# Layer norm factors applied in turned layout, key tiles moved ahead of outputs, and two more feed-forward steps in the linear-attention block

## The chip, the cores and the metric

One NeuronCore of one Trainium2 chip. The metric is the device time of the whole kernel in microseconds (us), median of the runs: 906.08 us for the kernel before (three runs, 906.05 to 906.83). TensorE (PE) multiplies matrices, VectorE (DVE), ScalarE (ACT) and GpSimd (POOL) do element work, SyncE (SP) issues the DMAs.

## The reference

The input x has 2 x 1024 tokens of 256 features. Four sub-layers follow each other: a mixture of 8 experts, linear attention with a feed-forward layer, masked softmax attention, and a mixture of 16 experts. The change touches only the second:

```
qkv = x @ Wqkv + bqkv;  q, k, v = split(qkv)
qp, kp = elu(q) + 1, elu(k) + 1
kv = sum over tokens of kp^T v;   k_sum = sum over tokens of kp
attn = (qp @ kv) / (qp @ k_sum + 1e-6)
y = layer_norm(x + attn) * g1 + b1          # "the first norm"
gate, up = y @ Wg + bg, y @ Wu + bu         # 256 -> 682
ffn = (silu(gate) * up) @ Wd + bd           # 682 -> 256
out = layer_norm(y + ffn) * g2 + b2
```

## The kernel before, in words

The 2048 tokens are 16 tiles of 128 rows; a batch is 8 tiles, and 4 tiles are a group of 512 tokens (4 groups). A matrix product in fp32 accuracy is made of three products of high and low parts (`PASSES`), so each operand is needed twice: `act_hi` (the value rounded, written by ACT) and `act_lo` (the rest, written by DVE). Both hold the activations in turned layout, features on the partitions and tokens along the row, while `y` holds them with tokens on the partitions.

The program is four blocks with a barrier between them, each a hand-written list of instructions per engine with semaphores: experts 1, linear attention (`stage_linear_attention`), feed-forward (`stage_feed_forward`), and attention with experts 2. Nothing reorders instructions: what is written ahead runs ahead on its engine.

Linear attention. SP issues the load of the query bias (L869), of Wg and Wu (L871), of the remaining groups and of biases. DVE adds up the experts' two rows of a token (`combine`, L1100), PE transposes them (L953), and then for each tile `project` (L919) gives keys and values, DVE makes keys (`bias` L1124, `keys` L1130 to L1135, `values_lo` L1140), PE adds them into the batch's key-value matrix two tiles later (`keys_values`, L933). `finish` (L1146 to L1149) makes that matrix ready for use. PE's `output(i)` (L945) is numerator and denominator of tile i; DVE divides and adds into y (L1158 to L1163), takes the norm's statistics (L1153, L1168, L763); ACT takes the root (L1057), DVE the shift (`norm`, L1237 and L1238), ACT applies both (L1245). The outputs of batch 0 (tiles 0 to 7) run beside the last four tiles of batch 1, those of batch 1 (tiles 8 to 15) after `finish(1)`. Then gain and bias of the first norm are applied to whole groups as rows: POOL for groups 0 and 1 (L1089, L1091), DVE for groups 2 and 3 (L1251, L1252). PE turns the group (`turn("r", g)`, L902), ACT and DVE write its high and low part (L997, L1106). `ff_up(s)` (L774) is one of 24 up-steps of the feed-forward layer (gate and up product of 128 hidden features for one group, 12 matmuls of 128x512); steps 0 and 1 stand in this block, the others in the next.

Feed-forward. For each step ACT applies Silu (L1406), DVE makes the hidden value and its high part (`hidden`, L1522, L1528), POOL the low part (L1292). A step's PSUM banks come free when `hidden` has read them. Between `hidden(2)` and `hidden(3)` DVE splits Wd (L758, L759). After six up-steps of a group, and two of the next, stands `down(g)` (L1327), 72 products into y (L1544). POOL adds the bias rows `bd` (L1479) and `be2` (L1484) between low parts.

## Time and profile before

| quantity | value |
|---|---|
| median of 3 runs | 906.08 us (906.05 to 906.83) |
| the profiled execution | 907.32 us, of which the span 905.6 us |
| PE busy | 824.6 us, 91% |
| DVE busy | 687.1 us, 76% |
| POOL busy | 406.7 us, 45% |
| ACT busy | 363.0 us, 40% |
| granted TensorE clock, mean | 0.958 |

Times below are microseconds from the start of the span. The profile lists instructions of one engine in order of time, with the idle time just ahead of them in brackets and what ended it. The linear-attention block runs from 299.1 to 413.9, the feed-forward block from there to about 528. Shares over the whole span say little here, since each block has its own limit: PE is almost always busy in the feed-forward block and idle for a third of the last stretch of linear attention.

### The profile page before, as it was taken

What the parts mean: (1) busy time and instruction counts of PE and PEld (TensorE: products, weight loads), DVE (VectorE), ACT (ScalarE), POOL (GpSimd) and SP (SyncE); (2) the same over time, 40 slices, a digit from 0 to 9 for tenths busy, and PEclk for the clock granted to TensorE, in tenths of its full rate; (3) what the DMA queues carried; (4) which work ended last, traced back from release to release, by engine and by line L of the source; (5) the groups of instructions that cost most, each with busy time, mean ns of one, the idle gap of its engine ahead of it and who ended that gap; (6) DMA issues with size and microseconds to landing.
All of it is one profiled execution on the core that took longest, in us unless ns stands there. A gap on an engine that the chain in (4) does not pass through costs nothing. (4 is left out here: it accounts for less than half of the span.)

```text
span 905.6 us, 17121 instructions
## 1 busy us (share of the span) xinstructions
PE 824.6 (91%) x5386; PEld 737.9 (81%) x5386; DVE 687.1 (76%) x1399; ACT 363.0 (40%) x722; POOL 406.7 (45%) x482
## 2 busy tenths in 40 slices
PE   7799999999996588677999989888999999999997
PEld 4799999999995367666888879766888888888887
DVE  4887888988884477976679779786777777776776
ACT  5466556666551555243322645783111111111110
POOL 4267778777784300044786427402232323233232
PEclk9699999999998799887999999999999999999999
DMA  8336412213611700005100020010010010010002
GB/s 288 107 118 200 140 46 82 92 43 133 198 47 50 233 1 1 1 0 181 43 1 1 1 71 2 1 35 1 18 35 17 17 35 17 17 35 17 17 0 93
DMA packets 45912, 55.20 MB, mean 61 GB/s; under 512 B 5166, under 2 KB 34920, under 8 KB 45864
## 3 DMA queue, kind: packets, MB, share of 16 engines
q1 hardware_dynamic: 41384, 43.59, 15.3%
q0 software_dynamic: 4032, 11.02, 4.0%
q8 instruction: 24, 0.39, 0.2%
q14 instruction: 24, 0.20, 0.1%
q10 hardware_dynamic: 448, 0.01, 0.0%
HBM read 47.00 MB, written 7.60 MB: 60 GB/s over the span
## 5 line engine op out<-in xcount | busy, mean ns | idle before, releaser
L2115 POOL TENSOR_TENSOR kTh<-at_acc,kTh 128x512 fp32r<-128x512 f32 x68 | 88.2, 1297 | 231.7 <-DVE kTh L2230 231.7
L1906 PE MATMUL psum<-act_hi,ff_w 128*128 128x512 f32 x544 | 180.0, 391 | 0.4 <-ACT at_acc L2071 0.4
L2071 ACT ACTIVATE at_acc<-psum 128x512 f32<-128x512 f32 x68 | 40.7, 600 | 237.3 <-PE psum L1906 237.3
L1906 PEld LDWEIGHTS psum<-act_hi,ff_w 128*128 128x128 f32 x544 | 102.4, 188 | 21.2 <-ACT at_acc L2071 0.8
L1947 PEld LDWEIGHTS psum<-ff_w,kTh 128*128 128x128 f32 x816 | 106.6, 191 | 8.8 <-DVE y L2311 3.1
L2311 DVE SCALAR_TENSOR_TENSOR y<-psum,ff_rawd,y 128x256 f32<-128x256 f32 x272 | 112.3, 475 | 0.2 <-PE psum L1947 0.2
L1947 PE MATMUL psum<-ff_w,kTh 128*128 128x256 f32 x816 | 108.6, 283 | 3.1 <-DVE y L2311 3.1
L1906 PE MATMUL psum<-act_lo,ff_w 128*128 128x512 f32 x272 | 106.8, 393 | 0.0
L470 ACT ACTIVATE e_u<-psum,e_bias 128x256 f32<-128x256 f32 x152 | 63.7, 472 | 94.8 <-PE psum L375 84.8
L2227 DVE TENSOR_TENSOR at_acc<-psum,at_acc 128x512 f32<-128x512 f32 x68 | 47.0, 691 | 70.9 <-PE psum L1906 58.5
L774 PE MATMUL psum<-act_hi,ff_w 128*128 128x512 f32 x192 | 63.5, 405 | 3.8 <-DVE ff_h32sb L1522 2.1
L1906 PEld LDWEIGHTS psum<-act_lo,ff_w 128*128 128x128 f32 x272 | 51.4, 189 | 8.1
L716 DVE CAST e_h2h<-e_u 128x512 fp32r<-128x512 f32 x38 | 35.6, 938 | 27.6 <-ACT e_u L470 27.4
L385 PE MATMUL psum<-e_w3h,e_h2h 128*128 (+1 forms) x160 | 47.9, 299 | 9.1 <-issue 8.7
L774 PEld LDWEIGHTS psum<-act_hi,ff_w 128*128 128x128 f32 x192 | 37.5, 195 | 13.2 <-DVE ff_h32sb L1522 3.3
L524 POOL DMA_INDIRECT y_rows<-e_yo,e_destnow x40 | 42.1, 1054 | 9.0 <-issue 8.7
L385 PE MATMUL psum<-e_w3l,e_h2h 128*128 (+1 forms) x160 | 45.8, 286 | 0.0
L385 PE MATMUL psum<-e_w3h,e_h2l 128*128 (+1 forms) x160 | 45.7, 286 | 0.0
L375 PE MATMUL psum<-e_h1h,e_w0l 128*128 128x256 f32 x160 | 45.2, 283 | 0.0
L375 PE MATMUL psum<-e_h1l,kTh 128*128 128x256 f32 x160 | 44.9, 281 | 0.0
L375 PE MATMUL psum<-e_h1h,kTh 128*128 128x256 f32 x160 | 44.6, 278 | 0.0
L546 POOL TENSOR_TENSOR e_h1l<-e_u,e_h1h 128x512 fp32r<-128x512 f32 x19 | 26.2, 1377 | 39.6 <-DVE e_h1h L716 39.6
(444 smaller groups left out, 2346.2 us busy)
## 6 DMA issues: line engine op xcount, KB each, us to landing
e_raw<-in_W SPq DMA_DIRECT2D x16, 512.0 KB, 6.7
e_raw<-in_W SPq DMA_DIRECT2D x8, 1024.0 KB, 6.0
v_tok<-in_xT SPq DMA_DIRECT2D x4, 512.0 KB, 9.9
y<-in_x SPq DMA_DIRECT2D x4, 512.0 KB, 10.5
y<-y_rows SPq DMA_DIRECT2D x4, 512.0 KB, 7.2
v_tok<-y_rows SPq DMA_DIRECT2D x4, 512.0 KB, 8.0
v_tok<-in_x SPq DMA_DIRECT2D x4, 512.0 KB, 7.5
e_raw<-in_w_gate SPq DMA_DIRECT2D x16, 128.0 KB, 2.1
```

The costliest lines, as they stand in the source:

```text
L375: last = pe.matmul(bank, wt[a][:, o + k * M1 + m * P:o + k * M1 + (m + 1) * P], src[b][:, k, :], start=k + i == 0, stop=k == kc - 1 and i ...
L385: last = pe.matmul(ps[4 if j * parts < TT else 0][:, j * D:(j + 1) * D], h2[a][:, k, j * P:(j + 1) * P], w3[b][:, bass.ds(slot, 1), k, :]. ...
L470: act.activation(u[:, c // 2, c % 2, :], ps[c // 2][:, (c % 2) * ET:(c % 2 + 1) * ET], ACT.Relu, bias=bias12[:, layer, e, c % MC:c % MC + ...
L524: pool.indirect_dma_start(out=y_rows, out_offset=bass.IndirectOffsetOnAxis(ap=of[:, j:j + 1], axis=0), in_=yo[:, j, :], in_offset=None).th ...
L716: dve.tensor_copy(h[0][:, k:k + 2, :], u[:, c, :, :]).then_inc(h_hi, 1)
L774: last = pe.matmul(bank, wt[a][:, k, m * P:(m + 1) * P], actT[b][:, k, g * GT:(g + 1) * GT], start=n == 0, stop=n == 3 * KC - 1)
L1906: last = pe.matmul(bank[:, :], e2_w[par][a][:, o + k * H2:o + (k + 1) * H2], actT[b][:, k, g * GT:(g + 1) * GT], start=n == 0, stop=n == 3 ...
L1947: last = pe.matmul(ps[4 + j][:, 0:D], hh[a][:, s % HS, j * P:(j + 1) * P], e2_w[par][b][:, OD:OD + D], start=n == 0, stop=n == 2)
L2071: act.activation(sl_sb[:, s % 2, :], ps[s % 2][:, :], ACT.Silu).then_inc(esil, 1)
L2115: pool.tensor_tensor(hh[1][:, s % HS, :], h32[:, s % 2, :], hh[0][:, s % HS, :], ALU.subtract).then_inc(hsp, 1)
L2227: dve.tensor_tensor(h32[:, s % 2, :], ps[2 + s % 2][:, :], sl_sb[:, s % 2, :], ALU.mult).then_inc(h32d, 1)
L2311: dve.scalar_tensor_tensor(out=y[:, i, :], in0=ps[4 + j][:, 0:D], scalar=comb[:, i, bass.ds(2 * t + out_s // G, 1)], in1=y[:, i, :], op0=A ...
```

## The change

1. Gain and bias of the first norm are no longer applied before the turn. PE turns the normed rows as soon as ACT has scaled them (`scaled`). ACT then writes `act_hi` with the 128 gains as per-partition scale and the biases as per-partition addend (`gained_high`), with a second instruction that gives the high part less the bias; DVE writes the low part from both (`gained_low`). The rows of y, which the residual needs, get gain and bias on POOL after the turn, tile by tile. The factors as columns are two more DMAs on SP behind the query bias, and DVE's first instruction of the block waits for them.
2. Only groups 0 to 2 are turned in the linear-attention block. Group 3 is normed, turned (`turn_first`) and gained in the feed-forward block, between steps 11 and 12.
3. Keys of tiles 14 and 15 stand on DVE ahead of most outputs of batch 0; `norm(0)` stands ahead of `finish(1)`; an early Sqrt on ACT brings its table in before `sums_out(1)`.
4. Four up-steps instead of two, and the first two hidden values with their low parts, stand in the linear-attention block (`EARLY`, `EARLY_HIDDEN`). Wd is loaded there too.
5. Buffers and PSUM banks are shared out anew; outputs 8 to 15 use banks 0, 1, 2, 0, 2, 0, 2, 0 and the turns banks 6 and 7.

```diff
+        EARLY, EARLY_HIDDEN = 4, 2
+        def gained_high(act, turn, bank, k, sl, cols, less, firm):
+            act.wait_ge(turned, turn)
+            act.activation(act_hi[:, k, sl], bank, ACT.Identity, scale=cols[:, 0, k:k + 1], bias=cols[:, 1, k:k + 1]).then_inc(firm, 1)
+            act.wait_ge(firm, turn - FIRST_TURN)
+            act.activation(less[:, k, :], act_hi[:, k, sl], ACT.Identity, bias=cols[:, 2, k:k + 1]).then_inc(hi_done, 1)
+        def gained_low(dve, turn, bank, k, sl, cols, less):
+            dve.wait_ge(hi_done, turn)
+            dve.scalar_tensor_tensor(out=act_lo[:, k, sl], in0=bank, scalar=cols[:, 0, k:k + 1], in1=less[:, k, :],
+                                     op0=ALU.mult, op1=ALU.subtract).then_inc(lo_done, 1)
...
                     sp.dma_start(bq[:, :], d["bq_cols"]).then_inc(bq_in, 16)
+                    for n, name in enumerate(("g1", "be1")):
+                        sp.dma_start(cols[:, n, :], d[name].rearrange("(k p) -> p k", p=P), allow_slow_non_contiguous=True).then_inc(cols_in, 16)
...
-                            pe.wait_ge(normed[g // OL], g % OL + 1)
+                            pe.wait_ge(scaled, g + 1)
...
-                    for i in range(NB, NT):
+                    for i in range(NB - 2, NB + 2):
                         output(i)
-                        if i % TG == TG - 1:
-                            turn("r", i // TG - OL)
+                    turn("r", 0)
+                    for i in range(NB + 2, NB + TG):
+                        output(i)
...
+                    ff_up(pe, ff_w, 0, ff_hps)
+                    turn("r", 1)
+                    pe.wait_ge(nuse, NB + 2)
+                    ff_up(pe, ff_w, 1, ff_hps)
+                    for i in range(NB + TG, NT):
+                        output(i)
+                    turn("r", 2)
+                    for s in range(2, EARLY):
+                        pe.wait_ge(ff_h32d, s - 1)
+                        ff_up(pe, ff_w, s, ff_hps)
...
-                        pool.tensor_tensor(y[:, sl, :], y[:, sl, :], group_rows(gb[:, 0, :]), ALU.mult).then_inc(gained, 1)
+                        pool.wait_ge(turned, n0 + NQ + (g + 1) * KC)
+                        for i in range(g * TG, (g + 1) * TG):
+                            last = pool.tensor_tensor(y[:, i, :], y[:, i, :], gb[:, 0, :], ALU.mult)
...
+                    dve.wait_ge(cols_in, 32)
+                    ch.link(dve.tensor_scalar(cols[:, 2, :], cols[:, 1, :], -1.0, None, ALU.mult))
                     dve.wait_ge(la_rin, 48)
                     ch.link(dve.tensor_scalar(bkv[:, 0:D], bkv[:, 0:D], 1.0, None, ALU.add))
                     combine(0)
...
                     for g in range(G):
-                        for m in range(2, FC):
+                        for m in range(2 if g else EARLY, FC):
                             up(g * FC + m)
+                        if g == 1:
+                            turn_first()
...
+                        if s == 13:
+                            pool.wait_ge(turned, n0)
+                            pool.tensor_tensor(rows1[:, 1, :], rows1[:, 1, :], down_bias, ALU.add).then_inc(wide, 1)
+                            for i in range(L1 * TG, NT):
+                                last = pool.tensor_tensor(y[:, i, :], y[:, i, :], rows1[:, 0, :], ALU.mult)
```

**DVE, last tiles of linear attention, before.** From the low part of tile 13's keys to those of tile 14 (`la_kt2`): the output of one tile is the four rows L1158, L1153, L1162, L1163.

```order
L1140 TENSOR_TENSOR la_kt2l<-psum,la_kt2h 128x256
L1158 TENSOR_SCALAR la_den<-psum 128x1
L1153 BN_STATS la_stats<-y 128x6
L1162 RECIPROCAL la_den<-la_den 128x1
L1163 SCALAR_TENSOR_TENSOR y<-psum,la_den,y 128x256
L1158 TENSOR_SCALAR la_den<-psum 128x1
L1153 BN_STATS la_stats<-y 128x6
L1162 RECIPROCAL la_den<-la_den 128x1
L1163 SCALAR_TENSOR_TENSOR y<-psum,la_den,y 128x256
L1153 BN_STATS la_stats<-y 128x6
L1168 BN_AGGR la_mv<-la_stats 128x2 x4
L763 TENSOR_SCALAR la_rstd<-la_mv 128x4
```

The same place now (lines of the changed kernel: keys L1188 to L1193, output L1216 to L1221, keys now kept in `pj_raw`):

```order
L1198 TENSOR_TENSOR la_kt2l<-psum,la_kt2h 128x256
L1188 SCALAR_TENSOR_TENSOR pj_raw<-pj_raw 128x256
L1192 CAST la_kt2h<-pj_raw 128x256
L1193 TENSOR_TENSOR la_kt2l<-pj_raw,la_kt2h 128x256
L1182 TENSOR_TENSOR pj_raw<-psum,rows 128x256
L1216 TENSOR_SCALAR la_den<-psum 128x1
L1211 BN_STATS la_stats<-y 128x6
L1220 RECIPROCAL la_den<-la_den 128x1
L1221 SCALAR_TENSOR_TENSOR y<-psum,la_den,y 128x256
L1198 TENSOR_TENSOR la_kt0l<-psum,la_kt0h 128x256
L1188 SCALAR_TENSOR_TENSOR pj_raw<-pj_raw 128x256
L1192 CAST la_kt0h<-pj_raw 128x256
```

Tile 14's keys stand ahead of outputs 2 and 3 and of group 0's statistics, and tile 15's behind output 2 alone.

**POOL, end of linear attention and start of feed-forward, before** (L1083 splits Wg and Wu, L1438 begins the feed-forward block):

```order
L1083 TENSOR_TENSOR ff_w<-ff_raw,ff_w 128x2x682 x2
L1089 TENSOR_TENSOR y<-y,rows 128x1024
L1091 TENSOR_TENSOR y<-y,rows 128x1024
L1089 TENSOR_TENSOR y<-y,rows 128x1024
L1091 TENSOR_TENSOR y<-y,rows 128x1024
L824 UNCONDITIONAL_BRANCH
L1438 UNCONDITIONAL_BRANCH
L1461 MEMSET ff_rawd 128x256
L1292 TENSOR_TENSOR qp<-ff_h32sb,qp 128x512 x2
```

and now (L1142 gain, L1146 bias, L1149 low part of the hidden values):

```order
L1136 TENSOR_TENSOR ff_w<-ff_raw,ff_w 128x2x682 x2
L1142 TENSOR_TENSOR y<-y,rows 128x256 x4
L1146 TENSOR_TENSOR y<-y,rows 128x256 x4
L1142 TENSOR_TENSOR y<-y,rows 128x256 x4
L1146 TENSOR_TENSOR y<-y,rows 128x256 x4
L1142 TENSOR_TENSOR y<-y,rows 128x256 x4
L1146 TENSOR_TENSOR y<-y,rows 128x256 x4
L1149 TENSOR_TENSOR qp<-ff_pair,qp 128x512 x2
L846 UNCONDITIONAL_BRANCH
L1525 UNCONDITIONAL_BRANCH
L1367 TENSOR_TENSOR qp<-ff_pair,qp 128x512 x2
```

Four whole-group instructions for two groups became 24 of one tile each for three groups, and two low parts stand behind them in the same block.

**DVE, start of the feed-forward block, before** (L824 ends the linear-attention block):

```order
L1106 TENSOR_TENSOR act_lo<-psum,act_hi 128x512 x4
L824 UNCONDITIONAL_BRANCH
L1512 UNCONDITIONAL_BRANCH
L1522 SCALAR_TENSOR_TENSOR ff_h32sb<-psum,ff_bu,ff_silusb 128x512
L1528 CAST qp<-ff_h32sb 128x512
...
L1522 SCALAR_TENSOR_TENSOR ff_h32sb<-psum,ff_bu,ff_silusb 128x512
L1528 CAST qp<-ff_h32sb 128x512
L758 CAST ff_wdh<-ff_rawd 128x1536
L759 TENSOR_TENSOR ff_wdl<-ff_rawd,ff_wdh 128x1536
```

and now:

```order
L1245 CAST qp<-ff_pair 128x512
L786 SCALAR_TENSOR_TENSOR act_lo<-psum,top,la_less 128x512 x2
L846 UNCONDITIONAL_BRANCH
L1605 UNCONDITIONAL_BRANCH
L1615 SCALAR_TENSOR_TENSOR ff_pair<-psum,ff_bu,ff_pair 128x512
L1621 CAST qp<-ff_pair 128x512
L758 CAST ff_wdh<-ff_rawd 128x1536
L759 TENSOR_TENSOR ff_wdl<-ff_rawd,ff_wdh 128x1536
L1615 SCALAR_TENSOR_TENSOR ff_pair<-psum,ff_bu,ff_pair 128x512
L1621 CAST qp<-ff_pair 128x512
```

The split of Wd stood behind the third hidden step of the block and now stands behind the first; in both kernels that is `hidden(2)`.

## Rows read from the trace of the kernel before

**Rows 1.** Stages: length; busy PE, PEld, DVE, ACT, POOL (instructions); clock; DMA share; GB/s

```profile
370.90:374.10 3.20, 3.20 (x22) 2.72 (x20) 3.03 (x16) 0.00 (x0) 0.00 (x0) 1.00 0.00 0
372.32:414.13 41.81, 25.45 (x130) 21.57 (x129) 33.69 (x106) 15.94 (x33) 9.52 (x5) 0.79 0.00 1
389.24:393.24 4.00, 1.54 (x12) 1.46 (x12) 3.82 (x16) 2.83 (x6) 3.92 (x3) 0.93 0.00 0
414.13:434.74 20.61, 19.71 (x73) 15.48 (x73) 12.28 (x16) 6.70 (x9) 15.05 (x16) 0.85 0.78 245
425.00:427.72 2.72, 2.72 (x14) 2.25 (x12) 0.16 (x1) 0.69 (x1) 2.72 (x4) 1.00 1.09 349
434.74:527.50 92.76, 88.72 (x538) 78.43 (x538) 74.59 (x155) 38.06 (x63) 60.85 (x84) 1.00 0.00 1
```

**Rows 2.** SP's queue at the block's start: start, length, line, DMA

```profile
299.11 0.35 SPq L869 DMA_DIRECT2D la_bq<-in_bq_cols  x1
299.51 0.43 SPq L871 DMA_DIRECT2D ff_raw<-in_Wg  x1
```

**Rows 3.** The DMA view of that start: KB each, us to landing

```profile
la_bq<-in_bq_cols SPq DMA_DIRECT2D x1, 1.0 KB, 1.7
```

**Rows 4.** DVE in linear attention, in order of time

```profile
299.76 1.67 DVE L1100 SCALAR_TENSOR_TENSOR y<-v_tok,top,y 128x256 f32<-128x256 f32 x4 [0.24 <-ACT y L992]
308.44 3.49 DVE L1112 SCALAR_TENSOR_TENSOR la_qrsb<-la_qesb,la_qrsb 128x512 f32<-128x512 f32 x2 [4.38 <-ACT la_qrsb L1005]
...
325.35 0.69 DVE L1112 SCALAR_TENSOR_TENSOR la_qrsb<-la_qesb,la_qrsb 128x512 f32<-128x512 f32 x1 [1.27 <-ACT la_qrsb L1005]
```

**Rows 5.** POOL at the block's start

```profile
305.08 5.70 POOL L1083 TENSOR_TENSOR ff_w<-ff_raw,ff_w 128x1364 fp32r<-128x1364 f32 x2 [4.01 <-ACT ff_w L1036]
```

**Rows 6.** PE from the block's start to the first down product

```profile
300.39 1.94 PE L953 MATMUL psum<-ident,y 128*128 128x128 f32 x8 [11.95 <-DVE y L1100]
...
375.69 0.39 PE L933 MATMUL psum<-la_kt2h 128*128 128x258 f32 x1 [1.56 <-DVE la_kt2l L1135]
...
378.97 0.45 PE L933 MATMUL psum<-la_kt0h 128*128 128x258 f32 x1 [2.29 <-DVE la_kt0l L1135]
...
383.35 0.55 PE L945 MATMUL psum<-la_kvh,qp 128*128 128x258 f32 x1 [2.85 <-DVE la_kvl L1149]
...
391.79 1.10 PE L902 MATMUL psum<-ident,y 128*128 128x128 f32 x8 [2.46 <-POOL y L1091]
...
414.13 0.77 PE L774 MATMUL psum<-act_hi,ff_w 128*128 128x512 f32 x1 [1.68 <-PEq L824]
...
434.74 0.36 PE L1327 MATMUL psum<-ff_wdh,qp 128*128 128x256 f32 x1 [0.36 <-POOL qp L1292]
```

**Rows 7.** DVE around the outputs of batch 1, and the split of Wd

```profile
381.93 0.48 DVE L1146 SCALAR_TENSOR_TENSOR la_kv<-rows,la_kv 128x256 f32<-128x256 f32 x1
...
387.12 2.19 DVE L1238 SCALAR_TENSOR_TENSOR la_shift<-la_mv,la_rstd 128x4 f32<-128x4 f32 x1
...
420.82 0.95 DVE L758 CAST ff_wdh<-ff_rawd 128x1536 fp32r<-128x1536 f32 x1
421.80 1.76 DVE L759 TENSOR_TENSOR ff_wdl<-ff_rawd,ff_wdh 128x1536 fp32r<-128x1536 f32 x1
```

**Rows 8.** ACT in the same stretch

```profile
384.71 2.07 ACT L1245 ACTIVATE y<-y,la_shift,la_rstd 128x256 f32<-128x256 f32 x4 [2.00 <-DVE la_shift L1238]
...
392.48 1.09 ACT L997 ACTIVATE act_hi<-psum 128x512 fp32r<-128x512 f32 x2 [1.05 <-PE psum L902]
```

**Rows 9.** POOL in the same stretch and in the feed-forward block

```profile
386.93 2.37 POOL L1089 TENSOR_TENSOR y<-y,rows 128x1024 f32<-128x1024 f32 x1 [76.15 <-ACT y L1245]
...
426.41 2.52 POOL L1292 TENSOR_TENSOR qp<-ff_h32sb,qp 128x512 fp32r<-128x512 f32 x2
...
440.73 2.82 POOL L1484 TENSOR_TENSOR v_tok<-v_tok,rows 128x256 f32<-128x256 f32 x4
...
452.91 4.96 POOL L1479 TENSOR_TENSOR y<-y,rows 128x256 f32<-128x256 f32 x4
```

More of the change, by code:

```diff
@@ L765, in ff_banks, with ff_gate @@
         def ff_banks(s):
-            return (ps[3 + 2 * s], ps[4 + 2 * s]) if s < 2 else (ps[s % 2], ps[2 + s % 2])
+            return ((ps[3], ps[4]), (ps[5], ps[1]))[s % 2] if s < EARLY else (ps[s % 2], ps[2 + s % 2])
+        EARLY, EARLY_HIDDEN = 4, 2
+        def ff_gate(act, s, gate, bg, ready, done):
+            act.wait_ge(ready, 2 * s + 1)
+            act.activation(gate[:, s % 2, :], ff_banks(s)[0], ACT.Silu, bias=bg[:, s % FC:s % FC + 1]).then_inc(done, 1)
+        def gained_high(act, turn, bank, k, sl, cols, less, firm):
[7 more added lines that the diff above has]
+                                     op0=ALU.mult, op1=ALU.subtract).then_inc(lo_done, 1)
+        FIRST_TURN = KC * G
         def ff_up(pe, w, s, done):
@@ L818, in stage_linear_attention @@
             kvout, kvps, kvdone, nps, nuse = sem("la_kvout"), sem("la_kvps"), sem("la_kvdone"), sem("la_nps"), sem("la_nuse")
-            rreq, root, densum, shifted, scaled, gained = (sem(f"la_{x}") for x in ("rreq", "root", "densum", "shifted", "scaled", "gained"))
-            normed = [sem(f"la_normed{n}") for n in range(2)]
+            densum, gained, cols_in = (sem(f"la_{x}") for x in ("densum", "gained", "colsin"))
+            mv, rstd, shift, cols, rreq, root, shifted, scaled, firm = norm1
             n0 = turns_done[0]
@@ L1029, in sums_out, with gained_hi @@
                             act.activation(kv32[:, c, :], ps[5 + c][:, 0:LW], ACT.Copy).then_inc(kvout, 1)
+                    def gained_hi(g):
+                        for k in range(KC):
+                            n = NQ + g * KC + k
+                            gained_high(act, n0 + n + 1, turned_bank(n), *split_at(n), cols, less, firm)
                     halves(0)
@@ L1053, in _ @@
                             halves(next_up(i))
+                    act.activation(early[:, :], ident[:, 0:1], ACT.Sqrt)
                     sums_out(1)
-                    for g in range(G):
+                    for g in range(TURNED):
                         act.wait_ge(rreq, g + 1)
@@ L1174, in norm, with gained_lo, hidden @@
                         shift_group(ch, g, mv, rstd, shift, root, shifted)
-                    def gain(g):
-                        dve.wait_ge(scaled, g + 1)
-                        gain_group(ch, y, g, gb[:, 0, :], group_rows(gb[:, 1, :])).then_inc(normed[1], 1)
+                    def gained_lo(g):
+                        for k in range(KC):
+                            n = NQ + g * KC + k
+                            gained_low(dve, n0 + n + 1, turned_bank(n), *split_at(n), cols, less)
+                    def hidden(s):
+                        dve.wait_ge(ff_sil, s + 1)
+                        dve.wait_ge(ff_hps, 2 * s + 2)
+                        dve.scalar_tensor_tensor(out=h32[:, s, :], in0=ff_banks(s)[1], scalar=ff_b[1][:, s:s + 1],
+                                                 in1=gate_sb[:, s, :], op0=ALU.add, op1=ALU.mult).then_inc(ff_h32d, 1)
+                        dve.wait_ge(ff_h32d, s + 1)
+                        dve.tensor_copy(hidden_home[0][:, s, :], h32[:, s, :]).then_inc(ff_hhi, 1)
+                    dve.wait_ge(cols_in, 32)
+                    ch.link(dve.tensor_scalar(cols[:, 2, :], cols[:, 1, :], -1.0, None, ALU.mult))
                     dve.wait_ge(la_rin, 48)
@@ L1637, in _ @@
                             norm(g - 1)
+                        if g == 1 and m == 2:
+                            shift_group(ch, L1, mv1, rstd1, shift1, root1, shifted1)
+                        if g == 2 and m == 0:
+                            for k in range(KC):
+                                gained_low(dve, n0 - KC + k + 1, ps[6 + k % 2], k, R1, cols1, less1)
                         if g in range(1, L1) and m == 4:
```

216 lines of the change are left out of this document (127 added, 89 removed).

## Prediction

> **What bounds the kernel now.** I read the page's shares first: PE is busy for 91% of the span, so a change can win only where PE waits. The stages [rows 1] say where: in the end of linear attention, 372.3 to 414.1, PE is busy 25.5 of 41.8 us and DVE 33.7; in the feed-forward block up to the first down product 19.7 of 20.6 us, and in the rest of it 88.7 of 92.8 us. So there are some 16 us of idle PE at the end of one block, 1 us at the start of the next, and 4 us spread over the rest. PE's list in order of time [rows 6] names the waits of the first stretch: 1.6 us for tile 14's keys, 2.3 us for tile 15's, 2.9 us for `finish(1)`, then a turn at 391.8 that waits for POOL's gain, and at 414.1 the barrier. All but the last are waits for DVE's or POOL's lists, which the change rewrites. While PE is idle the granted clock falls: it is 0.79 in this stretch and 0.85 in the next against 1.00, the 2.4 GHz level, afterwards [rows 1].
>
> Durations come from the profiled execution, 907.3 us (span 905.6), 1.2 us above the median 906.1; I take the change from its axis and subtract it from the median.
>
> **Start of the block.** DVE's `combine(0)` starts at 299.8 and PE's first turn at 300.4 [rows 4, 6]; PE has nothing else to do. Now DVE's first instruction waits for two DMAs of columns that SP issues behind the query bias. SP issues at 299.11 and takes 0.35 to 0.43 us for each [rows 2], so the second leaves at 299.9. The query bias lands 1.7 us after its issue [rows 3]; its 1 KB comes as 128 rows, the new ones bring the same bytes in twice as many pieces, so 1.7 to 2.5 us, and they land at 301.6 to 302.4. Then DVE starts at about 302.2 and PE at about 303.0: 2.6 us later. The Trainium skill, "DMA: Bandwidth & Descriptors", section "Anatomy of one DMA", puts the fixed part of a DMA at about 2.0 us; by that the columns would land at about 301.9 and this term would be 0.2 us smaller.
>
> Part of it returns. DVE's two L1112 take 3.5 us together beside POOL's split of Wg and Wu, which runs from 305.1 to 310.8, and 0.69 each alone [rows 4, 5]. Wg and Wu are issued 0.8 us later now, the split moves to some 306 to 311.6, and L1112 moves to 311, so most of the 2.1 us of stretch goes; how much of it is on the path I can't see. Between all of it and none I take 1.1. Term: +1.5 us, bounds 0 and +3.
>
> **End of linear attention.** On the axis of before:
> - An output of one tile is 1.0 us of DVE (389.24 to 393.24 holds four), and outputs 2 and 3 with the group's statistics fill 3.2 us from 370.9 on [rows 1]. Tile 14's keys pass all of that: PE's L933 for it goes from 375.7 [rows 6] to some 372.6. Tile 15's pass outputs 3, 4 and 5, and the statistics: 4 us, so the one of 379.0 goes to 375.0. `sums_out(1)` keeps its distance and no longer loads a table behind it. DVE still does outputs 3 and 4 and `norm(0)`, to 378.0, and then `finish(1)`, which began at 381.9 [rows 7]. The first product of batch 1, 383.35 before [rows 6], comes at 379.4: 3.9 us earlier.
> - The first turn waits for `scaled` alone, 2.07 us of ACT behind `norm(0)` [rows 8], and stands behind four outputs: at 382 to 383 instead of 391.8. `gained_high` is two ACT passes for each of two halves where it was one of 0.55 [rows 8], and DVE reaches `gained_low(0)` only behind outputs 5 to 7: low parts are there at 387.2, so up-step 0 runs from about 387 to 392.5 with the clock low.
> - From there DVE bounds: outputs 8 to 12 with `gained_low(1)`, then 13 to 15. Outputs 12 to 15 share two banks and wait for DVE twice, about 1.9 us. The third turn comes at 404 to 405, up-steps 2 and 3 follow and end at about 412.
> - The block ends when its last engine does. That is POOL: behind the third turn stand 8 row instructions and 2 low parts. A row of one tile is 0.71 (2.82 for 4), a low part 1.26 [rows 9], 0.74 with PE and DVE beside it: 8 x 0.74 + 2.5 = 8.5 us, so 413 to 414 and the next block's first matmul at 414.6, 0.5 us later than 414.13 [rows 6]. Before, POOL was idle at this place. Bounds: 411 if the turn comes at 401.5, 417 if the clock stays low for the second and third up-step.
>
> **First stretch of feed-forward.** Six up-steps stood there in 20.6 us [rows 1]: 2.72 us each at full clock (425.00 to 427.72 holds the 12 matmuls of one step [rows 1]), the first two slower, at a mean clock of 0.85. Four are left. Up-step 4 runs 414.6 to 417.4. Up-step 5 needs `hidden(3)` for its banks, and DVE has to do Silu's wait, `hidden(2)` (an instruction of 128x512 as L1112's, 0.69 [rows 4], and a cast), and the Wd split, 420.8 to 423.6 before, 2.7 us [rows 7], ahead of it. Nothing covers it now: it stood beside up-steps 4 and 5, whose banks were free. `hidden(3)` is read at about 420.3, so PE waits 3 us. Three up-steps take 8.2 us, and the idle stretch costs clock: 1 to 2.5 us. The first down product comes at 429.5 to 431.5, I take 430.7 against 434.74 [rows 6]. Together with the later block end this is the net gain of both stretches: -4.0 us; of that I give back 0.5 for the two POOL low parts that a later start would leave in the way. Term: -3.5, bounds -7 and 0.
>
> **Rest of feed-forward.** Added: 8 transposes, 1.10 us [rows 6] less their overlap, so 0.9. DVE gets two `gained_low` of the form of L1112, 0.69 [rows 4], ACT four passes and four norms, POOL 5 more row instructions, 3.5 us. DVE is busy 74.6 and POOL 60.9 of 92.8 us [rows 1], and both lists stand ahead of waits of PE for banks; POOL's four rows took 4.96 us beside DVE's whole-group gain instead of 2.82 [rows 9]. I put 1.0 us on these waits, bounds 0 and 2.1. Term: +1.9.
>
> Sum: 1.5 - 3.5 + 1.9 = -0.1 us: 906.0.
>
> **A rule on the shared port.** DVE's tiny L1238 (128x4) took 2.19 us and ended with POOL's L1089, 386.93 + 2.37 [rows 7, 9]. The Trainium skill, "SBUF — State Buffer", section "SBUF: two separate sides", says that a DVE instruction with two SBUF inputs and a GpSimd one exclude each other for the whole instruction; the trace agrees with its 2.19 us. A piece of one tile is 0.71 us, so one such stall costs 0.7 at most where it cost 2.0, but there are 24 pieces and 5 more in the feed-forward block. As a mechanism of this kernel: if five DVE instructions on the way to a bank meet one each, the feed-forward term grows by 3.5 us, the sum to +3.4, 909.5. By the page's rule that could be; the trace shows such DVE instructions beside POOL, at 434.7 to 527.5 with 60.9 us of POOL work, while PE waits only 4 us, so I give it 0.04 of the slower chance.
>
> **The rivals.**
> 1. *The waits saved are kept* (0.33 with other faster cases): PE's gaps shrink, the clock stays up in the up-steps that are now interleaved, the start is absorbed since DVE's L1112 stretch goes wholly, and the Wd split finds up-step 4 slow enough to cover it. For it: the 16 us of idle PE [rows 1], and three named waits of 6.7 us together that go. Against it: the block's end is set by POOL, which doesn't shift with them. 0 - 4.5 + 1.5 = -3: 903.1.
> 2. *The start's wait is passed on whole and POOL holds the barrier* (0.22, and 0.04 for the case above, 0.26 in all): the place is DVE's first instruction, +2.6 with nothing returned, because PE's projection behind it is a chain with DVE; then the last turn is 2.6 late too, POOL's 8.5 us end at 417, and up-step 5 pays the Wd split. 2.6 - 2.0 + 1.9 = +2.5: 908.6. It decides from the point where POOL's list ends over 2 us behind PE's up-step 3.
>
> My forecast stands between them (0.41): what the earlier keys and turns gain is used up by the start, by the wait at up-step 5 and by group 3's work in the next block. 906.0, own range 904.3 to 907.8.
>
> The measurement can tell 0.2%, 1.8 us, from no change. Faster by over 0.2% is 0.33, within it 0.41, slower 0.26. The range takes in both rivals with half their spread: 902.2 to 909.2.
>
> **What would show it.** Right: the first turn at about 303.0, DVE idle until the columns land; tile 15's L933 near 375 plus the shift of the start; batch 1's first product about 4 us earlier relative to it; the POOL low parts as the last instructions before the barrier; a PE wait of 2 to 4 us before the feed-forward block's second up-step, put down to `hidden`; 8 transposes in the middle of feed-forward and idle PE there of over 4 us. Wrong: POOL done before PE at the barrier; no wait at up-step 5; a stretch from 434 on that isn't longer than 92.8 us; or the clock in the interleaved up-steps at full speed from the first one on.

## The result and the profile after

The changed kernel takes 908.25 us (median of 20 runs, 906.97 to 910.11), the kernel before 906.07 us in the runs beside it (20 runs, 903.29 to 908.27). The ratio is 1.0028, 95% interval 1.0019 to 1.0036: slower by 0.28%, some 2.5 us. The prediction was 906.0 with no measurable change as the likeliest; 908.25 lies inside its range of 902.2 to 909.2, but the kernel moved, and it had only 0.26 for slower. The medians below are those of all executions; that of e12 and that of the kernel before beside e9 to e11 take in one far slower execution each (1028.65 and 941.69 us), which the ratios leave out.

The profiled execution took 907.73 us, its span 906.0. The block of linear attention begins at 296.58 there and at 299.11 before (first DMA of the block), 2.5 us earlier, though experts 1 is the same code; over all kernels below it began anywhere from 295.9 to 299.1, in no relation to the edits. So positions are told from the block's start, which leaves these sums:

| from the block's start, us | before | after | difference |
|---|---|---|---|
| first turn of PE | 1.28 | 4.44 | +3.16 |
| first product of batch 1 | 84.24 | 82.39 | -1.85 |
| up-step 0 | 98.94 | 93.53 | -5.41 |
| feed-forward block, first matmul | 115.02 | 118.03 | +3.01 |
| first down product | 135.63 | 134.27 | -1.36 |
| next block (attention), first matmul after its barrier | 229.29 | 230.96 | +1.67 |

What follows that barrier took 377.2 us before and 378.5 after. It is not the change: over the twelve experiments it is between 377.0 and 378.8, in no relation to the edits either.

The stages of the changed kernel, same columns as [rows 1], the first row over the same stretch as there and the last two from the block's barrier to the first down product and from there to the next block:

```profile
372.32:414.13 41.81, 30.63 (x142) 25.42 (x141) 28.59 (x102) 20.45 (x36) 19.66 (x26) 0.80 0.00 1
414.61:430.85 16.24, 12.92 (x49) 10.14 (x49) 10.18 (x12) 4.02 (x6) 11.01 (x11) 0.89 0.83 264
430.85:527.54 96.69, 90.73 (x548) 79.36 (x546) 79.11 (x159) 42.67 (x72) 65.26 (x91) 1.00 0.00 1
```

PE does 5 us more work in the end of linear attention than before [rows 1], as it should with two more up-steps, and still idles 11 of 42 us at a granted clock of 0.80. The last stage is 96.7 us where it was 93.7.

DMA of the columns (KB each, us to landing), DVE and POOL at the block's start, which answer to [rows 3 to 5]:

```profile
top<-in_be SPq DMA_DIRECT2D x1, 1.0 KB, 2.4
```

```profile
299.86 0.17 DVE L1248 TENSOR_SCALAR top<-top 128x2 f32<-128x2 f32 x1 [14.21 <-DMA top<-in_be]
300.39 1.67 DVE L1158 SCALAR_TENSOR_TENSOR y<-v_tok,top,y 128x256 f32<-128x256 f32 x4
...
309.08 2.94 DVE L1170 SCALAR_TENSOR_TENSOR ff_pair<-ff_pair 128x512 f32<-128x512 f32 x2 [4.38 <-ACT ff_pair L1050]
```

```profile
305.18 5.69 POOL L1136 TENSOR_TENSOR ff_w<-ff_raw,ff_w 128x1364 fp32r<-128x1364 f32 x2 [6.38 <-ACT ff_w L1086]
```

The columns land 2.4 us after their issue, 3.3 us behind the block's start, and DVE's first instruction waits for them. POOL's split begins 8.6 us behind the block's start; before it was 6.0 [rows 5]. So it did not stay behind while DVE came later, it moved with DVE, and L1170 (L1112 before) meets it again: 2.94 us where it was 3.49 [rows 4].

PE from the block's start to the first down product, as [rows 6]:

```profile
301.02 1.94 PE L990 MATMUL psum<-ident,y 128*128 128x128 f32 x8 [15.84 <-DVE y L1158]
...
374.56 0.39 PE L970 MATMUL psum<-la_kt0h 128*128 128x258 f32 x1 [1.78 <-DVE la_kt0l L1193]
...
378.97 0.36 PE L982 MATMUL psum<-la_kvh,qp 128*128 128x258 f32 x1 [1.98 <-DVE la_kvl L1207]
...
388.66 0.58 PE L982 MATMUL psum<-la_kvh,qp 128*128 128x258 f32 x1 [3.87 <-DVE y L1221]
...
390.11 0.63 PE L796 MATMUL psum<-act_hi,ff_w 128*128 128x512 f32 x1
...
402.66 0.39 PE L982 MATMUL psum<-la_kvh,qp 128*128 128x258 f32 x1 [1.60 <-DVE y L1221]
...
414.61 0.47 PE L796 MATMUL psum<-act_hi,ff_w 128*128 128x512 f32 x1 [0.33 <-PEq L846]
...
420.93 0.65 PE L796 MATMUL psum<-act_hi,ff_w 128*128 128x512 f32 x1 [3.32 <-DVE ff_pair L1615]
...
430.85 0.28 PE L1398 MATMUL psum<-ff_wdh,qp 128*128 128x256 f32 x1
```

The row at 388.66 is the one to look at. It is `output(11)`, which needs PSUM bank 0 back from `output(8)`. DVE's list there:

```profile
383.99 0.17 DVE L763 TENSOR_SCALAR top<-top 128x4 f32<-128x4 f32 x1
385.17 0.75 DVE L786 SCALAR_TENSOR_TENSOR act_lo<-psum,top,la_less 128x512 fp32r<-128x512 f32 x1 [1.01 <-ACT la_less L781]
386.59 0.75 DVE L786 SCALAR_TENSOR_TENSOR act_lo<-psum,top,la_less 128x512 fp32r<-128x512 f32 x1 [0.67 <-ACT la_less L781]
...
388.12 0.48 DVE L1221 SCALAR_TENSOR_TENSOR y<-psum,la_den,y 128x256 f32<-128x256 f32 x1
...
392.64 0.17 DVE L763 TENSOR_SCALAR top<-top 128x4 f32<-128x4 f32 x1
399.13 0.16 DVE L1216 TENSOR_SCALAR la_den<-psum 128x1 f32<-128x1 f32 x1 [6.32 <-PE psum L982]
399.93 1.40 DVE L786 SCALAR_TENSOR_TENSOR act_lo<-psum,top,la_less 128x512 fp32r<-128x512 f32 x2
401.24 0.17 DVE L1308 RECIPROCAL top<-top 128x4 f32<-128x4 f32 x1
...
417.48 2.73 DVE L759 TENSOR_TENSOR ff_wdl<-ff_rawd,ff_wdh 128x1536 fp32r<-128x1536 f32 x1
```

`output(8)` ends with the row at 388.12. It stands behind group 0's low parts, for which DVE waits twice on ACT (1.01 and 0.67). Then DVE idles 6.3 us until PE, late and for most of up-step 0 at the low clock (0.63 for a matmul of 128x512), reaches `output(12)`; and behind that stand group 1's low parts and `norm(2)` (401.24), on which the last turn and all that follows it depend.

### The profile page after: what moved, and what is told of

The parts are those of the page before. It is cut to its first block and busy times, and to the rows that moved or that the text cites. A ratio compares the mean times of both kernels' runs of the same rounds, so it can differ in the third digit from the quotient of the medians.

```text
span 906.0 us, 17156 instructions
## 1 busy us (share of the span) xinstructions
PE 822.7 (91%) x5386; PEld 735.6 (81%) x5386; DVE 686.0 (76%) x1396; ACT 369.4 (41%) x731; POOL 417.1 (46%) x507
## 5 line engine op out<-in xcount | busy, mean ns | idle before, releaser
L2213 POOL TENSOR_TENSOR kTh<-at_acc,kTh 128x512 fp32r<-128x512 f32 x68 | 88.1, 1296 | 233.3 <-DVE kTh L2328 233.3
L2004 PE MATMUL psum<-act_hi,ff_w 128*128 128x512 f32 x544 | 180.4, 392 | 0.4 <-ACT at_acc L2169 0.4
L796 PE MATMUL psum<-act_hi,ff_w 128*128 128x512 f32 x192 | 65.9, 417 | 5.6 <-DVE ff_pair L1615 4.1
L716 DVE CAST e_h2h<-e_u 128x512 fp32r<-128x512 f32 x38 | 37.7, 993 | 25.1 <-ACT e_u L470 24.8
L1142 POOL TENSOR_TENSOR y<-y,rows 128x256 f32<-128x256 f32 x12 | 8.6, 751 | 83.4 <-PE psum L939 83.4
```

The costliest lines, as they stand in the source:

```text
L716: dve.tensor_copy(h[0][:, k:k + 2, :], u[:, c, :, :]).then_inc(h_hi, 1)
L796: last = pe.matmul(bank, wt[a][:, k, m * P:(m + 1) * P], actT[b][:, k, g * GT:(g + 1) * GT], start=n == 0, stop=n == 3 * KC - 1)
L2004: last = pe.matmul(bank[:, :], e2_w[par][a][:, o + k * H2:o + (k + 1) * H2], actT[b][:, k, g * GT:(g + 1) * GT], start=n == 0, stop=n == 3 ...
L2213: pool.tensor_tensor(hh[1][:, s % HS, :], h32[:, s % 2, :], hh[0][:, s % HS, :], ALU.subtract).then_inc(hsp, 1)
```

## The experiments

Each was timed in 5 rounds beside the kernel before. Ratios are against it; "stretch" is from the block's start to the next block in the profile (229.3 before, 231.0 changed). On e1, e2 and e3: theory S says that the start's wait is the loss, rival F that it is made in the feed-forward block.

A stretch is read from one execution of each kernel, and executions of one kernel differ. e1, e5, e6, e8 and e11 run the same code up to the feed-forward barrier, and it came 114.5 to 117.4 us behind the block's start: 114.8 in e1, where the granted clock over the 15 us from 84 to 99 behind the start was 0.89, and 117.4 in e11, where it was 0.69. So a stretch names the place of a wait, but a difference of 3 us between two stretches shows no gain by itself. What an edit is worth is told from the ratios.

| kernel | median us | ratio, 95% interval | stretch |
|---|---|---|---|
| changed | 908.25 | 1.0028, 1.0019 to 1.0036 | 231.0 |
| e1 late wait for columns | 906.01 | 1.0001, 0.9988 to 1.0014 | 227.7 |
| e2 before + columns and wait | 910.08 | 1.0041, 1.0025 to 1.0057 | 233.2 |
| e3 Wd split one step later | 906.75 | 1.0012, 0.9999 to 1.0025 | 229.0 |
| e4 before + key order | 904.87 | 0.9984, 0.9970 to 0.9999 | 227.5 |
| e5 e1 + Wd split in parts | 903.41 | 0.9979, 0.9967 to 0.9991 | 226.8 |
| e6 e1 + group 3's queues | 904.53 | 0.9993, 0.9982 to 1.0004 | 226.9 |
| e7 e1 with two early steps | 904.85 | 0.9999, 0.9987 to 1.0010 | 228.1 |
| e8 e5 and e6 | 903.07 | 0.9973, 0.9961 to 0.9984 | 225.0 |
| e9 e8 + output(8) first | 898.92 | 0.9927, 0.9905 to 0.9949 | 222.7 |
| e10 e9 + low parts ahead | 896.49 | 0.9909, 0.9887 to 0.9931 | 219.0 |
| e11 e1, light group 3 | 906.48 | 1.0011, 0.9995 to 1.0027 | 230.3 |
| e12 changed + order of e10 | 901.74 | 0.9964, 0.9950 to 0.9978 | 226.0 |

**e1: the wait for the columns moved back**

```diff
-                    dve.wait_ge(cols_in, 32)
-                    ch.link(dve.tensor_scalar(cols[:, 2, :], cols[:, 1, :], -1.0, None, ALU.mult))
...
+                        if i == 1:
+                            dve.wait_ge(cols_in, 32)
+                            ch.link(dve.tensor_scalar(cols[:, 2, :], cols[:, 1, :], -1.0, None, ALU.mult))
```

> The changed kernel with DVE's wait for the columns of g1 and b1 (and the instruction that negates b1) moved from the head of its list to behind the keys of tile 0; the DMAs stay where they are. Theory S (the start's wait is the loss): the first turn comes about 3.1 us earlier against the block's start (1.3 us behind it instead of 4.4), and the whole kernel is 2.3 to 3.1 us faster than the changed one: 905.3 to 906.1, level with the kernel before. Rival F (the loss is made in the feed-forward block, and the start is absorbed, since DVE and POOL overlap there): the turn comes earlier but tile 15's keys come at the same distance from the block's start as before, and the time stays within 1 us of 908.3.

The first turn came 1.28 us behind the block's start, the stretch fell by 3.25 us and the ratio by 0.27%, 2.4 us. As theory S expected, the kernel is level with the one before.

Inside the block the delay is not constant. The first product of batch 1 stands at 82.4 behind the start in the changed kernel and in e3, and at 80.1 to 80.9 in e1 and e5 to e11, which have the same code up to there but for the wait: some 1.8 us of the 3.16 are left there, and 1.3 had returned (in e12, at 83.5, next to nothing had). At the barrier it is 118.0 against e1's 114.8 again. That second part goes with the clock, 0.67 and 0.68 in the changed kernel and e3 over the 15 us from 84 on, 0.89 in e1; but e11, which has no such wait either, had 0.69 there and its barrier at 117.4, so these single executions don't show that the wait made it. What is shown is the price in time, 2.4 us here.

**e2: the same wait in the kernel before**

```diff
+                    for n, name in enumerate(("g1", "be1")):
+                        sp.dma_start(xcols[:, n, :], d[name].rearrange("(k p) -> p k", p=P), allow_slow_non_contiguous=True).then_inc(cols_in, 16)
...
+                    dve.wait_ge(cols_in, 32)
+                    ch.link(dve.tensor_scalar(xcols[:, 2, :], xcols[:, 1, :], -1.0, None, ALU.mult))
```

> The kernel before with that one part added: two column DMAs on SP behind the query bias, and DVE waiting for them ahead of its first instruction. Theory S: 2.5 to 3.1 us slower than before, ratio 1.0028 to 1.0034, as POOL's split and DVE's L1112 still meet or not. Rival F: at most 1 us slower, ratio up to 1.001.

Slower by 0.41%, 3.7 us, which is more than theory S's 2.5 to 3.1, though they lie within the interval. The stretch grew by 3.9 us: the wait (first turn at 4.41 instead of 1.28) and 0.8 more. At the first product of batch 1 only 1.8 us of it were left here too (86.0 against 84.2). DVE, POOL and ACT of e2, whose block starts at 297.92:

```profile
310.39 2.94 DVE L1115 SCALAR_TENSOR_TENSOR la_qrsb<-la_qesb,la_qrsb 128x512 f32<-128x512 f32 x2 [4.38 <-ACT la_qrsb L1008]
```

```profile
306.49 5.69 POOL L1086 TENSOR_TENSOR ff_w<-ff_raw,ff_w 128x1364 fp32r<-128x1364 f32 x2 [6.61 <-ACT ff_w L1039]
```

```profile
304.09 1.08 ACT L1000 ACTIVATE act_hi<-psum 128x512 fp32r<-128x512 f32 x2 [4.45 <-PE psum L956]
305.07 2.57 ACT L1039 ACTIVATE ff_w<-ff_raw 128x1364 fp32r<-128x1364 f32 x2
```

ACT rounds the weights (L1039), which starts POOL's split, directly behind the first turn's high part (L1000), and that waits for the turn. So the split hangs on the turn and not on the loads.

**e3: the Wd split behind hidden(3)**

```diff
-                        if s == 2:
+                        if s == 3:
                             dve.wait_ge(d_in, 32)
```

> The changed kernel with the split of Wd on DVE one hidden step later, behind hidden(3) instead of hidden(2). Theory S: the wait of PE for hidden(3), 3.3 us at up-step 5, goes, and another of 1 to 2 us appears at up-step 6 for hidden(4), behind the split; the first down product comes 1.5 to 2.5 us earlier and the time falls by 1 to 2.5 us, to 905.8 to 907.3. Rival F: all of the 3.3 us and the low clock behind it come back, 904.5 to 905.5. A third way: the split lands where POOL's low parts stand and nothing is gained (908.3).

The stretch fell by 2.0 us and the ratio by 0.16%, 1.5 us. PE's wait in e3:

```profile
424.64 0.50 PE L796 MATMUL psum<-act_hi,ff_w 128*128 128x512 f32 x1 [2.22 <-DVE ff_pair L1615]
```

3.3 us became 2.2, one step later, and the granted clock stayed at 1.00 behind it. As theory S expected: the wait is DVE's 3.7 us of split (0.95 and 2.75) between two hidden values, wherever it stands in one piece.

**e4: the key order alone**

```diff
-                        if i:
+                        if 0 < i < NT - 1:
                             keys(i - 1)
+                        if i == NT - 1:
+                            output(2)
                         values_lo(i)
+                        if i >= NT - 2:
+                            keys(i)
...
+                    output(3)
+                    output(4)
+                    norm(0)
                     finish(1)
```

> The kernel before with one part of the change alone: the keys of tiles 14 and 15 ahead of outputs 2 and 3 onwards on DVE, PE's outputs 6 and 7 behind the last keys, norm(0) ahead of finish(1), an early Sqrt on ACT. The turns, gains and up-steps stay as before. Expected by both theories: the first product of batch 1 comes 3.9 us earlier. If the end of the block follows the chain from there (POOL's two whole-group gains of group 0, turn, outputs, DVE's gains), the block ends 2 to 3.9 us earlier and the time is 902.2 to 904.2. If norm(0), done earlier, does not bring POOL's gain forward or the clock is lower in the stretch, the gain is 0 to 1 us.

Faster by 0.16%. The first product of batch 1 came 3.8 us earlier (80.5 behind the block's start), and 1.8 us were left at the block's end. The 2 to 3.9 us that the first case expected were missed in time (1.4 us), and the 0 to 1 us of the second too.

**e5: the Wd split in three parts**

```diff
-                        if s == 2:
+                        if s in (3, 4, 5):
                             dve.wait_ge(d_in, 32)
-                            weights_split(dve, ch, [(rawd[:, :, :], wd[0][:, :, :], wd[1][:, :, :])], wsp)
+                            c = slice(2 * (s - 3), 2 * (s - 2))
+                            ch.link(dve.tensor_copy(wd[0][:, c, :], rawd[:, c, :]))
+                            last = dve.tensor_tensor(wd[1][:, c, :], rawd[:, c, :], wd[0][:, c, :], ALU.subtract)
```

> The kernel of e1 (late wait for the columns), with the split of Wd cut in three parts of 128x512, one each behind hidden(3), hidden(4) and hidden(5). Theory: PE's wait of 3.5 us at up-step 5 goes and none over 0.5 us takes its place, and the clock stays up behind it, so the first down product comes 3 to 4.5 us earlier against the block's start (131.0 in e1, so 126.5 to 128) and the time is 902 to 903. Rival (e3 showed it: the wait only moves, and POOL's low parts beside the split stretch it): a wait of 1 to 2.4 us remains, 904 to 905.

The first down product came at 128.8 behind the start, 2.3 us earlier, while e5's block had ended 1.0 later than e1's; from barrier to down product it is 13.0 us instead of 16.2. Two waits of 0.7 remain, and one of 1.0 came in behind the first down product: from there to the next block e5 takes 98.1 us where e1 takes 96.7, so 1.8 of the 3.2 us are left. 903.4 is between the two expectations.

**e6: two pieces of work moved away from group 3's**

```diff
-                COUNTED = {g * FC + m: (g - 1) * 4 + n for g in (1, 2) for n, m in enumerate((0, 2, 3, 5))}
-                BIASED, XBIASED = {3: 0, 7: 1, 11: 2, 17: 3}, {5: 0, 9: 1, 15: 2, 19: 3}
+                COUNTED = {g * FC + m: (g - 1) * 4 + n for g in (1, 2) for n, m in enumerate((0, 2, 3, 5) if g == 1 else (1, 2, 3, 5))}
+                BIASED, XBIASED = {3: 0, 7: 1, 11: 2, 20: 3}, {5: 0, 9: 1, 15: 2, 19: 3}
```

> The kernel of e1 with two instructions groups moved in the feed-forward block: one of the eight mask counts on DVE, which stands between group 3's low parts and the down adds, goes behind the adds (behind step 13 instead of 12), and POOL's bias rows of group 3 go from step 17 to step 20, away from DVE's ranking of key blocks. Theory Q (the 3 us that the rest of the feed-forward block grew by is 0.9 of transposes and 2 of queueing on DVE and POOL): the waits of 0.71 and 0.86 us in the second and third down product shrink or go, the stretch from the first down product to the next block (96.7) falls by 1 to 1.5 us. Rival W (it is the work itself: transposes, passes, 5 more row instructions): no change over 0.3 us.

From down product to next block it went from 96.7 to 96.2, which neither side expected. PE's waits at the third down product (0.27 and 0.70 in the changed kernel) went; the one of 0.56 at the second stayed (0.54), since the cast of a hidden value ahead of the adds took 1.53 us there instead of 0.43; and the one of 0.78 for the hidden value of an up-step grew to 1.38. What the four bias rows had cost at step 17 is seen in the changed kernel. DVE, POOL, PE:

```profile
488.76 1.59 DVE L1691 TENSOR_SCALAR ff_raw<-ff_raw 128x8 f32<-128x8 f32 x1
```

```profile
485.74 3.06 POOL L1565 TENSOR_TENSOR y<-y,rows 128x256 f32<-128x256 f32 x4
488.76 1.30 POOL L1367 TENSOR_TENSOR qp<-ff_pair,qp 128x512 fp32r<-128x512 f32 x1
```

```profile
491.59 0.38 PE L1398 MATMUL psum<-ff_wdh,qp 128*128 128x256 f32 x1 [0.70 <-DVE y L1637]
```

and the same DVE instruction in e6:

```profile
484.99 0.22 DVE L1692 TENSOR_SCALAR ff_raw<-ff_raw 128x8 f32<-128x8 f32 x1
```

An instruction on 128x8 takes 1.59 us beside POOL's rows and low part and 0.22 where they are moved away, and PE's adds stand behind it. So queueing behind group 3's work cost 1 us of PE's waits here, and e6 nets half of that because another wait grew.

**e7: two early steps instead of four**

```diff
-        EARLY, EARLY_HIDDEN = 4, 2
+        EARLY, EARLY_HIDDEN = 2, 0
...
-                    hidden(0)
                     output(NB + TG + 3)
-                    hidden(1)
```

> The kernel of e1 with two up-steps in the linear-attention block instead of four, and no hidden values there (EARLY 2, EARLY_HIDDEN 0): steps 2 and 3 and hidden(0), hidden(1) go back to the feed-forward block, where the split of Wd then stands beside up-steps again. If the early steps are worth their place: the block ends 4 to 5 us earlier but the first down product comes 1 to 3 us later than in e1, time 907 to 909. Rival: they only moved time (the split's wait of 3.5 us and the table load eat them), and the time is within 1 us of e1's 906.0, or below it.

No difference from e1 in time, as the rival expected; the 0.4 us in the stretch is less than two executions differ by, and the barrier came 2.9 us earlier, not 4 to 5. PE at e7's barrier, which falls 112.0 us behind its start where e1's falls at 114.8:

```profile
408.69 0.77 PE L796 MATMUL psum<-act_hi,ff_w 128*128 128x512 f32 x1 [6.04 <-PEq L846]
```

Without the two steps PE only waits longer for POOL's rows, which end at 408.35. In the changed kernel they fill that wait and pay for it with the Wd split's 3.3.

**e8: e5 and e6 together**

```diff
...
+                        if s in (3, 4, 5):
...
+                BIASED, XBIASED = {3: 0, 7: 1, 11: 2, 20: 3}, {5: 0, 9: 1, 15: 2, 19: 3}
```

> The edits of e5 and e6 together on the kernel of e1. If the three causes (start, Wd split, queues behind group 3's work) are separate and add up: 901 to 902.5, faster than both kernels, ratio about 0.9955. If they overlap: 903 to 904.5.

The stretch fell by 2.7 us against e1; e5 and e6 alone gave 0.9 and 0.8. The time, 903.07, is no better than e5's within the intervals, and above the 901 to 902.5 of adding up.

**e9: output(8) ahead of group 0's low parts**

```diff
+                    output(NB)
                     gained_lo(0)
                     norm(1)
-                    for i in range(NB, NB + TG + 1):
+                    for i in range(NB + 1, NB + TG + 1):
                         output(i)
```

> The kernel of e8, with DVE's output(8) moved ahead of the low parts of group 0: that is what PE's output(11) waits for (3.9 us in the changed kernel), and DVE idles 1.7 us there for ACT. Theory D (DVE's order holds the end of the block): output(11) comes 3 us earlier, up-step 0 starts when group 0's low parts are there, 2 to 2.8 us earlier, and the block ends 1.5 to 2.8 us earlier: 900.3 to 901.6. Rival P (POOL's row instructions or ACT's passes hold it): the block ends less than 1 us earlier, 902 to 903.

**e10: group 1's low parts and norm(2) ahead of output(12)**

```diff
-                    for i in range(NB + 1, NB + TG + 1):
+                    for i in range(NB + 1, NB + TG):
                         output(i)
                     gained_lo(1)
                     norm(2)
+                    output(NB + TG)
```

> e9, and also group 1's low parts and norm(2) ahead of output(12) on DVE, which idles there for 6 us. Theory D: the third turn comes 1.5 to 2 us earlier still and with it POOL's last instructions and the end of the block: 898.5 to 900.5. Rival: output(12) is delayed by as much as the norm is brought forward, or PE's outputs 14 and 15 set the turn, and there is no change against e9 over 0.5 us.

Two moves of one line took 2.3 and 3.8 us out of the stretch, and 4.2 and 2.4 us out of the medians (0.46% and 0.18% by the ratios). Theory D holds, but both times lie below its ranges, and in e9 up-step 0 came 0.8 us earlier, not 2 to 2.8. Of the 3.8 us in e10's stretch 1.0 were there at up-step 0 already (88.1 against 89.1), which the second move cannot have brought. e10 is the fastest kernel of the study, 0.91% faster than before. Its stage and its PE (block start 297.85):

```profile
372.32:414.13 41.81, 32.77 (x168) 26.39 (x169) 35.23 (x108) 22.15 (x38) 24.64 (x31) 0.96 0.14 37
```

```profile
384.54 0.39 PE L982 MATMUL psum<-la_kvh,qp 128*128 128x258 f32 x1 [1.03 <-DVE y L1221]
385.95 0.47 PE L796 MATMUL psum<-act_hi,ff_w 128*128 128x512 f32 x1 [0.42 <-DVE act_lo L786]
...
406.38 0.47 PE L796 MATMUL psum<-act_hi,ff_w 128*128 128x512 f32 x1 [1.36 <-PEq L846]
```

The wait of 3.9 us is 1.0. The granted clock of the stretch is 0.96 instead of 0.80, and up-step 0 runs at the 2.4 GHz level (0.39 for a matmul of 128x512), where the changed kernel ran most of it at 1.2 (0.63, at 390.11). In e9 up-step 0 was at 2.4 too, but over 372 to 410 the clock was still 0.78, against 0.96 in e10. POOL is the last engine at the barrier: PE waits 1.36 us for it.

**e11: group 3's low parts and rows on two columns**

```diff
-                                gained_low(dve, n0 - KC + k + 1, ps[6 + k % 2], k, R1, cols1, less1)
+                                dve.scalar_tensor_tensor(out=act_lo[:, k, L1 * GT:L1 * GT + 2], in0=ps[6 + k % 2][:, 0:2],
...
-                                last = pool.tensor_tensor(y[:, i, :], y[:, i, :], rows1[:, 0, :], ALU.mult)
+                                last = pool.tensor_tensor(y[:, i, 0:2], y[:, i, 0:2], rows1[:, 0, 0:2], ALU.mult)
```

> The kernel of e1, where group 3's low parts on DVE and its five row instructions on POOL in the feed-forward block work on two columns only: left out are the other columns' low parts, gains and bias, so the output differs for group 3. The transposes and ACT's passes stay. The stretch from the first down product to the next block is 96.7 in e1 and 93.7 before. Theory Q (queueing behind this DVE and POOL work is 2 of the 3 us): it falls to 94.5 to 95.2. Rival W (transposes and ACT's passes): it stays above 96.

From down product to next block: 96.7 us, as in e1, so the time did not follow the work that was taken out, and theory Q's 94.5 to 95.2 were missed. (That e11's whole stretch is 2.6 us longer than e1's is made before the barrier, where both are the same code.) PE's waits are those of the changed kernel within 0.04 us. At the second down product (0.53), DVE and POOL of e11:

```profile
459.43 1.46 DVE L1622 CAST qp<-ff_pair 128x512 fp32r<-128x512 f32 x1
460.81 0.74 DVE L1638 TENSOR_TENSOR y<-psum,y 128x256 f32<-128x256 f32 x2
```

```profile
456.34 3.00 POOL L1566 TENSOR_TENSOR y<-y,at_acc 128x256 f32<-128x256 f32 x4
459.30 1.30 POOL L1368 TENSOR_TENSOR qp<-ff_pair,qp 128x512 fp32r<-128x512 f32 x1
```

The cast ahead of the down adds takes 1.46 us beside POOL's low part and ends with it, within 0.3 us; in the changed kernel it took 0.43 at this place. The adds, and PE behind them, wait for that. So the two low parts gave 1.07 us (1.40 to 0.33), and the cast took 1.03 back, because POOL's piece now falls upon it. At the third down product nothing changed: the four bias rows of step 17 are not among those made light, and the instruction on 128x8 still took 1.59 us. e11 therefore shows that making these pieces light brings nothing as the lists stand, and not that group 3's work has no price.

**e12: the order of e10 on the changed kernel alone**

The diffs of e9 and e10 on the changed kernel, nothing else.

> The changed kernel with the order of DVE from e9 and e10 alone: output(8) ahead of group 0's low parts, and group 1's low parts with norm(2) ahead of output(12). The wait for the columns, the split of Wd and the queues of group 3 stay as the change has them. e8 to e10 fell by 6.0 us in the stretch from the block's start to the next block. If the order is a cause of its own, this kernel falls by 5 to 6 us against the changed one, to 902 to 903.5, faster than before by 0.3 to 0.5%. If it only pays once the start's wait is gone, it falls by less than 3 us.

The stretch fell by 5.0 us and the ratio from 1.0028 to 0.9964, 5.8 us, with the start's wait (first turn at 4.34) and the Wd wait (3.3 us) still there. The order is a cause of its own and the largest.

## Why the prediction was wrong

Point by point, in microseconds of the profile:

- **Start, +1.5 forecast; by time 2.4 us (e1) and 3.7 us (e2).** The failed step is "Wg and Wu are issued 0.8 us later now, the split moves to some 306 to 311.6 ... so most of the 2.1 us of stretch goes". The split moved by 2.6 us and not by 0.8, because ACT starts it behind the first turn, and it met L1170 again: 2.94 us for 3.49, so 0.55 of the 2.1 went. I had read when POOL ran and not what released it, though [rows 5] names it: ACT, L1036. The first turn was 3.16 late (2.6 forecast; the DMA took 2.4 us from an issue that itself came at 0.9). The 2.0 us that the prediction quotes from the Trainium skill, "DMA: Bandwidth & Descriptors", section "Anatomy of one DMA", stand there for DMAs that GpSimd issues; SP issued these, and they took 2.1 and 2.4. Of the delay 1.3 us had returned at the first product of batch 1 in three executions of four, near the 1.1 that I had taken for another reason, but the times, 2.4 and 3.7 with intervals of some 1.5 either way, do not show a return, and by e2's the term was more than twice too small.
- **End of linear attention and first stretch of feed-forward, -3.5.** Measured against the later first turn: -1.36 - 3.16 = -4.5. The size was right within 1 us. The earlier keys came, and brought 1.1 us more than forecast (first product of batch 1 79.2 behind the shifted start, 80.3 forecast). The barrier came at 114.9 (115.5 forecast) with POOL near its end, the wait at up-step 5 was 3.3 (3 forecast), put down to `hidden`. But up-step 0 came at 90.4 and not at 88: I sized the two banks of outputs 12 to 15 and not bank 0 of `output(11)`, which waits for `output(8)` behind the low parts.
- **Rest of feed-forward, +1.9.** Measured +3.0, the second term that was too small. The transposes are there (1.08 us, 0.9 forecast). PE's waits, counted from the start of one matmul to the start of the next and beyond the usual distance, grew by 1.6 us (5.7 to 7.3) and not by 1.0; by the stage rows, which count a matmul longer behind a wait, PE idles 1.0 us more (4.9 to 6.0) and is busy 2.0 more. I put the waits down to the amount of DVE's and POOL's added work. e6 and e11 show that it is where POOL's pieces fall: a DVE instruction on 128x8 took 1.59 us for 0.22 beside the bias rows of step 17, and a cast 1.46 for 0.43 beside a low part. Why the wait of 0.78 grew to 1.38 in e6 stays open, and so do some 0.3 us of the 3.0.
- **Sum.** +1.5 - 3.5 + 1.9 = -0.1 against 3.16 - 4.5 + 3.0 = +1.67 in the profile. The ratio says +2.5 with an interval of 1.7 to 3.3. The slower rival, start passed on whole (2.6 - 2.0 + 1.9 = +2.5), is near it, and I gave it 0.22. The start is its, but its sum agrees by luck: it has -2.0 where -4.5 was measured and +1.9 where it was +3.0. "POOL holds the barrier" was not decisive in the changed kernel (PE waits 0.33 us there), and is in e7 and e10. Of the signs of being wrong none came clearly: the wait at up-step 5 was there, the last stage grew, the clock was low, and POOL's low parts ended with PE (414.2).
- **The rule on the shared port.** L1238's kind of stall is short now at its old place (0.36 for 2.19), but group 3's took 1.28 us in the feed-forward block, from 472.24 to 473.52, beside POOL's low part from 472.20 to 473.51. That agrees with the rule of the Trainium skill, "SBUF — State Buffer", section "SBUF: two separate sides", that such a pair excludes each other for a whole instruction: L1309 has two SBUF inputs. Whether PE waited for it no row says.

```profile
472.24 1.28 DVE L1309 SCALAR_TENSOR_TENSOR ff_rawd<-ff_rawd 128x4 f32<-128x4 f32 x1
```

```profile
472.20 1.31 POOL L1367 TENSOR_TENSOR qp<-ff_pair,qp 128x512 fp32r<-128x512 f32 x1 [3.53 <-DVE qp L1621]
```

The DVE instructions that met POOL ahead of a wait of PE were others, with one SBUF input each: L1691 on 128x8 (1.59 us) and, in e6 and e11, the cast of hidden values (1.53 and 1.46). Rows show their prices and no row shows why they stall. The prediction had 0.04 for a case of this kind, five stalls and +3.5 us; it was not that much, but it was on the path.

The change does contain its gain: the key order is worth 1.8 us of stretch and 1.4 us of time (e4); that the four early steps are worth anything is not shown (e7 against e1). What hid the gain were a wait put at the head of the block for data needed 85 us later, and an order on DVE in which outputs whose banks PE waits for stand behind instructions that wait for ACT.

## What to carry to other kernels

When a wait is put at the head of a queue, count its whole price unless you can name work that does not hang on it: follow the releasers of the work that is to absorb it, not its times. In a queue written by hand, look for a short instruction that frees a buffer and stands behind one that itself waits; here two such places were worth 5.8 us (e12), more than any other single edit. Cut long weight preparations into pieces that fit between the steps of the pipeline. And before a stretch of one execution is called a gain, look at a second kernel with the same code there.
